# Half of the first butterfly level by an accumulating DMA in a gated BitNet feed-forward kernel

## What is computed

```python
gate = bitlinear(x, w_gate)          # act_quant(x) times ternary weights, 512 -> 2048
up = bitlinear(x, w_up)
intermediate = jax.nn.silu(gate) * up
return h_bitlinear(intermediate, w_down)   # act_quant(fwht(.)), 2048 -> 512
...
def fwht(x):                         # n = 2048, eleven levels of (a + b, a - b)
    h = 1
    while h < n:
        x = x.reshape(-1, n // (2 * h), 2, h)
        a, b = (x[..., 0, :], x[..., 1, :])
        x = jnp.stack([a + b, a - b], axis=-2).reshape(-1, n)
        h *= 2
```

## Time and profile before

| | |
|---|---|
| Median of three runs | 469.24 us (468.75 to 471.29) |
| Span of the profiled execution | 468.3 us |
| TensorE matmul busy | 412.0 us, 88% |
| VectorE busy | 397.7 us, 85% |
| ScalarE busy | 329.6 us, 70% |
| GpSimd busy | 155.0 us, 33% |
| Butterfly instructions on VectorE | 128, 153.6 us |
| Chain that ended last | TensorE 64%, VectorE 10%, GpSimd 9%, issue 7% |

### The profile page before, as it was taken

How to read it: one execution, slowest core, us unless ns; L and a number is a source line. 1 busy time by engine, 2 the same in 40 slices (tenths; PEclk the granted TensorE clock), 3 DMA queues, 4 the chain that set the end, 5 groups by cost and what they waited for, 6 DMA issues and landing times.

```text
span 468.3 us, 8176 instructions
## 1 busy us (share of the span) xinstructions
PE 412.0 (88%) x2490; PEld 292.0 (62%) x2491; DVE 397.7 (85%) x668; ACT 329.6 (70%) x518; POOL 155.0 (33%) x199
## 2 busy tenths in 40 slices
PE   0068999999999988597999999999999999999793
PEld 0046777877787734375766666666766667666571
DVE  5783589669859879899999999999999999999682
ACT  4415544854673562467999999989999999987761
POOL 0587021121211406434424424533433442432101
PEclk9998899999999999989999999999999999999898
DMA  7787025205310000000000000000000000000001
GB/s 286 283 300 233 6 91 180 90 0 178 112 69 1 1 1 0 0 1 1 1 24 22 0 22 22 0 22 24 23 0 22 22 0 22 24 1 24 22 24 45
DMA packets 5318, 25.80 MB, mean 55 GB/s; under 512 B 1072, under 2 KB 1072, under 8 KB 3248
## 3 DMA queue, kind: packets, MB, share of 16 engines
q1 hardware_dynamic: 2736, 17.13, 10.2%
q0 software_dynamic: 2560, 8.39, 5.1%
HBM read 21.33 MB, written 4.19 MB: 55 GB/s over the span
## 4 chain that ended last, share of the span: by engine, by line
PE 64%; DVE 10%; POOL 9%; issue 7%; ACT 4%; DMA 3%; DVEq 1%; SPq 0%; POOLq 0%; ACTq 0%
PE bank L467 11%; PE bank L380 11%; PE bank L484 11%; PE bank L445 10%; PE bank L452 10%; PE bank L352 7%; PE bank L477 3%; POOL xs L255 2%; POOL item_var L263 2%; DMA stage<-ctx_dram 2%; DMA xs<-x_dram,order 1%; POOL item_rstd L266 1%; DVE bfly L1045 1%; DVE scratch L886 1%; DVEq L861 1%
## 5 line engine op out<-in xcount | busy, mean ns | idle before, releaser
L1045 DVE TENSOR_TENSOR bfly<-prod 128x1024 f32<-128x1024 f32 x64 | 76.4, 1217 | 0.1
L467 PE MATMUL bank<-cst,mT 128*128 128x128 f32 x512 | 69.8, 280 | 5.7 <-ACT mT L655 5.7
L467 PEld LDWEIGHTS bank<-cst,mT 128*128 128x128 f32 x512 | 66.4, 194 | 12.9 <-ACT y L669 4.8
L445 PE MATMUL bank<-wq,xqT 128*128 128x512 bf16 x256 | 65.9, 380 | 2.1 <-ACT xqT L617 1.3
L484 PE MATMUL bank<-wq,yqT 128*128 128x512 bf16 x256 | 66.4, 383 | 0.0
L452 PE MATMUL bank<-wq,xqT 128*128 128x512 bf16 x256 | 65.7, 379 | 0.5 <-DVE prod L1037 0.5
L308 POOL TENSOR_SCALAR out_s<-yamax,down_c 128x1 f32<-128x1 f32 x14 | 31.9, 2282 | 58.0 <-DVE yamax L1028 58.0
L697 ACT ACTIVATE sg<-bank,gate_s 128x512 f32<-128x512 f32 x64 | 44.0, 687 | 8.7 <-PE bank L445 7.0
L655 ACT ACTIVATE mT<-bank 128x512 f32<-128x512 f32 x64 | 38.2, 596 | 14.8 <-PE bank L352 14.7
L1037 DVE TENSOR_TENSOR prod<-bank,sg 128x512 f32<-128x512 f32 x64 | 43.4, 680 | 5.3 <-ACT sg L697 3.5
L647 ACT ACTIVATE y<-y,yqs 128x512 f32<-128x512 f32 x56 | 40.4, 722 | 10.2 <-POOL yqs L310 10.2
(11 more groups left out here) (140 smaller groups left out, 855.8 us busy)
## 6 DMA issues: line engine op xcount, KB each, us to landing
stage<-ctx_dram SPq DMA_DIRECT2D x4, 1024.0 KB, 10.1
stage<-wgate_dram SPq DMA_DIRECT2D x4, 1024.0 KB, 4.8
stage<-wup_dram SPq DMA_DIRECT2D x4, 1024.0 KB, 4.7
stage<-wdown_dram SPq DMA_DIRECT2D x4, 1024.0 KB, 4.8
cst<-consts_dram SPq DMA_DIRECT2D x1, 338.0 KB, 2.9
xs<-x_dram,order POOLq DMA_INDIRECT x16, 4.1
out_dram<-res,order POOLq DMA_INDIRECT x16, 3.0
idt<-ids_dram SPq DMA_DIRECT2D x1, 8.0 KB, 1.8
```

The source lines that it names most:

```text
L445: last = nc.tensor.matmul(ps_gate[:, :], xqT[:, b, c, :], wq[:, 0, c * F + 512 * n:c * F + 512 * (n + 1)], start=(c == 0), stop=(c == DC - 1))
L467: last = nc.tensor.matmul(bank_[:, c * P:(c + 1) * P], mT[:, n % 2, c, :], had, start=True, stop=True)
L1045: return tt(dst[:, :, half], src[:, :, 0], src[:, :, 1], ALU.subtract if half else ALU.add)
```

## The change

`prod` gives way to `wide`, which has three half tiles of eight chunks: the multiplies of quarters 0 and 1 write the first, those of quarters 2 and 3 the second. The first level to be done is now the one that pairs chunks 8 apart. Its difference, first half minus second, is formed by VectorE into the third half (`half_difference`, at the end of body t). Its sum is formed in place: a DMA that GpSimd issues adds the second half to the first, in SBUF (`half_sum`, at the head of turn t+1 of GpSimd's loop). The remaining three levels, with chunks 1, 2 and 4 apart, run over the sum half and the third half. They stand in quarters 1, 2 and 3 as before; quarter 0 has none. Level 1 waits for the DMA. The last level's two instructions now each write half of both halves of `mixed`, so TensorE waits for the second of them before quarter 1.

```diff
-        prod = sb("prod", [P, 2, FC, P], F32, late)
+        wide = sb("wide", [P, 2, 3, FC // 2, P], F32, late)
...
+            def half_sum(t):
+
+                b = t % 2
+                pool.wait_ge(diff_set, t + 1)
+                pool.dma_start(wide[:, b, 0, :, :], wide[:, b, 1, :, :], accum_op=ALU.add).then_inc(sum_done, 16)
+
             for t in range(NT + 4):
+                if 1 <= t <= NT:
+                    half_sum(t - 1)
                 if 3 <= t <= NT:
                     y_int_scale(t - 3)
...
             def mix_transposes(t, b, n, bank_):
-                if n % 2 == 0:
-                    pe.wait_ge(mixed_set, t * 2 + (n // 2 + 1))
+                if n < 2:
+                    pe.wait_ge(mixed_set, t * 2 + (n + 1))
...
-                tt(prod[:, b, 4 * n:4 * n + 4, :].rearrange("p c m -> p (c m)"), ps_up[n % 2][:, :],
-                   sg[:, n % 2, :], ALU.mult).then_inc(prod_set, 1)
+                tt(wide[:, b, n // 2, 4 * (n % 2):4 * (n % 2) + 4, :].rearrange("p c m -> p (c m)"),
+                   ps_up[n % 2][:, :], sg[:, n % 2, :], ALU.mult).then_inc(prod_set, 1)
+
+            def half_difference(t, b):
+
+                dve.wait_ge(prod_set, t * NQ + NQ)
+                tt(wide[:, b, 2, :, :], wide[:, b, 0, :, :], wide[:, b, 1, :, :], ALU.subtract).then_inc(diff_set, 1)
 
             def butterfly(b, n, half):
 
-                src = (prod[:, b, :, :], bfly[:, :, :], prod[:, b, :, :], bfly[:, :, :])[n]
-                dst = (bfly[:, :, :], prod[:, b, :, :], bfly[:, :, :], mixed[:, b, :, :])[n]
-                src, dst = (a.rearrange("p (g two h) m -> p g two (h m)", two=2, h=2 ** n) for a in (src, dst))
-                return tt(dst[:, :, half], src[:, :, 0], src[:, :, 1], ALU.subtract if half else ALU.add)
+                halves = wide[:, b, 0:3:2, :, :]
+                flat = bfly[:, :, :].rearrange("p (a c) m -> p a c m", a=2)
+                last = mixed[:, b, :, :].rearrange("p (a c) m -> p a c m", a=2)
+                src, dst = ((halves, flat), (flat, halves), (halves, last))[n - 1]
+                src, dst = (a.rearrange("p a (g two h) m -> p a g two (h m)", two=2, h=2 ** (n - 1)) for a in (src, dst))
+                return tt(dst[:, :, :, half], src[:, :, :, 0], src[:, :, :, 1], ALU.subtract if half else ALU.add)
...
-                    if bf:
-                        if n == 0:
-                            dve.wait_ge(prod_set, (t - 1) * NQ + NQ)
+                    if bf and n >= 1:
+                        if n == 1:
+                            dve.wait_ge(sum_done, t * 16)
                         else:
                             s.wait(bfly_step)
...
+                    if gu and n == 3:
+                        half_difference(t, b)
                     if rnd and n == 0:
                         y_clip(t - 3, o, s, y_step)
```

More of the change, by code:

```diff
@@ L224, in gated_moe_bitnet_kernel @@
         res_free = sem("res_free")
+        diff_set, sum_done = sem("diff_set"), sem("sum_done")
         block = persistent.enter_context(nc.Block())
```

## The result

The changed kernel takes **512.88 us** (median of four runs, 511.55 to 514.32) where the kernel before took 469.0 us beside it (468.21 to 471.29). The ratio is 1.090, with a 95% interval from 1.085 to 1.095. The forecast was 519 us, its range 484 to 568. The profiled execution has a span of 510.5 us, against 468.3 before: 42.2 us to account for. From here on *after* is the changed kernel.

The account below looks back on a forecast made before the run. TensorE was taken to bound the steady body, with VectorE 0.2 us behind; the DMA wait makes VectorE the bound. Body terms sum to +49.3 us on the 468.3 us span, 517.6, plus 0.9 to the median: 519 us, range 484 to 568.

Parts of the forecast that it names:

- TensorE bounds the steady body, and work taken off VectorE gains nothing there: Steady body of 16.84 us: TensorE sets the pace, VectorE idles only 0.21 us, so relieving VectorE gains nothing.
- The moved wait on mixed and the deeper patterns cost nothing: TensorE's wait moved to quarter 1 and six butterflies with one more pattern dimension: both costed at nothing.
- A loop through GpSimd and the DMA, with a cover of 1.92 us: VectorE ahead of level 1: path 6.4 us less 1.92 us of VectorE work before the wait, stall 4.5 us.
- GpSimd's rest and dispatch, 1.18 us: GpSimd between difference and DMA: 1.0 us for the three ffn scales, 0.18 us to start the DMA.
- Issue to landing, 5.2 us: Accumulating DMA of 512 KB: 2.25 us fixed plus 1 MB read at 3.0 us per MB, 5.2 us.
- Bodies 3 to 14: 20.0 us each, +38.1: Twelve steady bodies, VectorE setting the pace with the stall: 240.0 us against 201.95.
- Bodies 1 and 2: +4.2 and +2.9: First bodies, with less VectorE work ahead of the wait: stalls 6.4 and 5.8 us, bodies 19.6 and 19.5 us.
- Body 16: yqs 2.2 us later: Last butterflies: level 1 and yrec wait for the sum landing at 433.3, so yqs ends at 435.9, against 433.69.
- the clock falls in the pause: Rival: TensorE's clock drops after a 3.2 us pause in quarter 2, 0.6 us a body, 529 us; chance 0.07.
- the addition costs no more than a copy: Rival: the DMA lands in 3.0 to 3.75 us, giving 484 to 496 us; chance 0.17.
- Slower than two reads: Rival: addition halves the DMA's rate once more, landing 8.25 us, 568 us; chance 0.21.
- Hidden: Rival: path under 3.26 us, landing under 2.1 us, body stays 16.84 us, 466 to about 469 us; chance 0.05.

Follow-up runs that it names:

- the split order: Changed kernel with levels 1 to 3 split by half, the difference half first, the DMA wait behind quarter 1's multiply: 467.16 us, ratio 0.996 to the kernel before.
- its twin with VectorE's sum: Same half-by-half order, difference half first, but VectorE forms the sum half behind the difference, without a DMA: 468.3 us, ratio 0.997 to the kernel before.
- VectorE's sum: Changed kernel with VectorE forming the sum half in place right behind the difference, no DMA, levels not split: 470.72 us, ratio 1.003 to the kernel before.
- the kernel with the filled pause: Changed kernel with sixteen extra transposes, changing no value, in TensorE's quarter 2 pause: 507.28 us, ratio 1.085 to the kernel before.
- the half copy: Changed kernel with GpSimd's DMA a plain copy of 256 KB, nothing added, so output differs from the reference's: 473.0 us.
- the DMA-first kernel: Half-by-half order, difference half first, with GpSimd's accumulating DMA issued ahead of the ffn scales: 469.3 us, ratio 0.999 to the kernel before.

## Why the prediction was right, and where it was off

- **TensorE bounds the steady body, and work taken off VectorE gains nothing there.** Right within 0.1 us: with a butterfly a body less on VectorE the split order has a body of 16.84 us, its twin with VectorE's sum one of 16.93. Their ratios to before don't differ.
- **The moved wait on mixed and the deeper patterns cost nothing.** Right within 0.3% (VectorE's sum, 470.72 us, 0.09 us a steady body), and the butterflies are at 1215 to 1218 ns.
- **A loop through GpSimd and the DMA, with a cover of 1.92 us.** Right in form and in size: the stall is 3.14 us, plus 0.34 us before the multiply, where the sg came later than in the earlier trace rows. Together they are 3.48 us where path less cover gives 3.77; small gaps between the rows hold the remaining 0.3.
- **GpSimd's rest and dispatch, 1.18 us.** 1.09, by two errors that cancel. ffn_var took 1.11 us beside the difference, much as the earlier trace rows said, and not 0.18. ffn_shift ended 1.15 us behind the difference where 1.0 was forecast, and the DMA's issue began 0.06 us before that end, where a dispatch of 0.18 had been put.
- **Issue to landing, 5.2 us. This is the step that was mis-sized: 4.6 us.** The slope of 3.0 us per MB came from loads out of HBM and the fixed 2.25 us from a store into HBM. Within SBUF the copy's slope is 2.4 us per MB and its fixed part 1.8 us. The rule "an addition reads both operands, so count its bytes twice" gave the right ratio: 5.2 us per MB against 2.4. Of the 0.6 us, the slope makes 0.4 and the fixed part 0.2. 0.6 us over sixteen tiles is 9.6 us, more than the whole miss of 6 us.
- **Bodies 3 to 14: 20.0 us each, +38.1.** 19.2 us each where the clock held, +29.8 in all, 8.3 less. Twelve bodies of 19.2 would be 9.6 less: the landing makes 7.2 of that, the shorter rest 1.1, small gaps the remainder. The first and the last of the twelve were shorter still, 18.44 and 18.56 us, which I had not foreseen. The three long bodies gave 2.4 us back and body 4 0.4.
- **Bodies 1 and 2: +4.2 and +2.9.** +3.3 and +1.9, both by the shorter landing (4.7 and 4.6 us) and a few tenths.
- **Body 15: +1.9.** +2.1. The DMA started 0.39 us behind the difference and not 0.80, and landed after 5.0 us.
- **Body 16: yqs 2.2 us later.** It is. Its rows in after, VectorE's and GpSimd's:

```profile
464.79 1.23 DVE L1052 TENSOR_TENSOR wide<-wide 128x1024 f32<-128x1024 f32 x1
...
471.97 1.23 DVE L1061 TENSOR_TENSOR bfly<-wide 128x1024 f32<-128x1024 f32 x1 [4.32 <-DMA wide<-wide]
...
466.31 0.88 POOL L333 DMA_DIRECT2D wide<-wide  x1 [6.10 <-DVE wide L1052]
...
473.37 1.16 POOL L311 TENSOR_SCALAR yqs<-yrec,up_s 128x1 f32<-128x1 f32 x1 [5.36 <-DVE yrec L1041]
```

  From the start of the difference to the end of yqs it is 9.74 us. Before, from the first butterfly at 426.17 to the end of yqs at 433.69 it was 7.52. The parts were off and cancelled: the DMA started 0.39 us behind the difference, not 0.80, and landed 5.66 us later, not 5.2. That these cancelled is luck: in the kernel with the filled pause the same DMA landed after 4.5 us. The other 1.3 us of the stretch lie behind the last res, in unchanged code.
- **Not in the sum: 1.8 us before body 1.** The code there is unchanged. The ten other kernels with that code start body 1 between 174.6 us (the half copy) and 177.0 (VectorE's sum), a spread of 2.4 us. After's 177.83 lies 0.8 us above it, and I can't say why.
- **So the closeness is in part luck.** The sum gave +49.3 us and the profiled execution has +42.2. The terms of the sum alone were 10 us too high; the clock's and body 4's shares are already in that. 3.1 us ahead of body 1 and behind the last res, which were not in the sum and are in unchanged code, brought the two nearer.
- **TensorE busy for 84% of bodies 3 to 14, a stall of 4.5 us.** 89%, and 3.1 us. The butterflies are 112, 16 of them differences, as said.
- **The rival "the clock falls in the pause".** It was put as an alternative; it came as well as the forecast, in three of nine bodies, 0.8 us each, together 2.4 us where it had been put at 10. It should have stood as a term with a share, not as a case of its own.
- **The rival "the addition costs no more than a copy".** Fell by the copy of the same bytes: 3.0 against 4.6 us. **"Slower than two reads"** fell too, in time: 4.6 us against its 8.25. **"Hidden"** was out of reach for this order: it needs a path of 3.26 us, and the fixed part and GpSimd's rest alone are near that.

## What to carry to other kernels

Before handing work from a busy engine to a DMA, find out who sets the body: here the engine relieved was 0.2 us from being the bound, but was not it, so even when the transfer was hidden the gain was at most 0.1 us a body. A DMA in a loop costs its whole path (queue ahead of it, dispatch, fixed part, bytes, an addition's bytes twice), less only what the waiting engine has ahead of the wait. To hide one, put work that doesn't need it between its start and its wait, as the split by halves does, rather than trying to make the transfer shorter.

## What the runs showed of the hardware that I had not expected

- A copy of 512 KB within SBUF lands in 3.0 us when GpSimd issues it and in 2.9 us when SyncE does; 256 KB take 2.4 us. A store of 256 KB to HBM took 3.0 us.
- The issue of an adding DMA holds GpSimd for 0.91 us, that of a plain copy for 0.63 us, and neither changes with half the bytes. SyncE's issue of the copy takes 0.46 us.
- ffn_var takes 1.11 us where it runs beside the difference, and 0.18 us where it starts just behind y_max (the DMA-first kernel). ffn_rstd takes 0.57 us beside y_max, and 1.41 us beside two butterflies (at 192.77 us of the trace before). The Trainium skill (SBUF — State Buffer, Who interferes with whom) states that a VectorE instruction with two inputs in SBUF holds up a GpSimd instruction that reads SBUF, and one with one input, outside VectorE's two-port modes, does not; by that, the trace agrees.
- The landings aren't all alike. The last one of after took 5.6 us and the longest of the split 5.9, against a median of 4.6. The last half copy took 4.6 against 2.4, and SyncE's last copy 5.0 against 2.9. In each of these a packet of an instruction queue (q8 or q14) went through the DMA engines between issue and landing. That queue's row from the last DMA of after, 466.0 to 472.5 us (packets, MB, share of 16 engines), and from the one of body 4, 235.5 to 241 us, which landed after 5.0 us:

```profile
q8 instruction: 1, 0.02, 1.3%
```

```profile
q14 instruction: 2, 0.02, 0.9%
```

  Of the 144 landings in the nine traces with such a DMA, 18 are 0.3 us or more above the median of their trace, and all 18 have such a packet. 119 have none, and none of these is more than 0.2 us above. Seven have one and are not long. That the packet is the cause is likely by this and not shown.
- Three of seven pauses of 2.16 to 2.21 us of TensorE were followed by the lower clock, and four were not. The length of the pause alone doesn't tell which.
